# One adaLN block on one core: the distance bias of the maximum is made by GpSimd alone from the fourth head on

## The reference

```python
scores = jnp.einsum('bihd,bjhd->bhij', q, k)
pos = jnp.arange(t)
alibi = -jnp.abs(pos[None, :] - pos[:, None]).astype(scores.dtype)
scores = scores + slopes[:, None, None] * alibi
probs = jax.nn.softmax(scores.astype(jnp.float32), axis=-1).astype(scores.dtype)
out = jnp.einsum('bhij,bjhd->bihd', probs, v).reshape(b, t, e)
```

## Time and profile before

| | |
|---|---|
| timed executions | 583.66, 583.89, 580.77 us |
| median | 583.66 us |
| profiled execution | span 580.7 us; its own time is taken as the 580.77 us above |
| TensorE busy | 457.7 us, 79% of the span |
| VectorE, ScalarE, GpSimd busy | 325.7, 255.4, 247.4 us |
| granted TensorE clock, mean of the span | 0.901 of full speed |

### The profile page before, as it was taken

The page is one execution under the profiler, slowest core; times in us unless marked ns, Lnnn a source line. Parts: engine busy times, 40 slices in busy tenths (PEclk is TensorE's granted clock), DMA queues, the critical chain, the costliest instruction groups (busy, mean ns, idle before and its releaser), DMA issues.

```text
span 580.7 us, 9712 instructions
## 1 busy us (share of the span) xinstructions
PE 457.7 (79%) x2167; PEld 233.9 (40%) x2168; DVE 325.7 (56%) x1035; ACT 255.4 (44%) x407; POOL 247.4 (43%) x351
## 2 busy tenths in 40 slices
PE   4988689999999999999988637976787777677800
PEld 1673133333333333333436623644444444344400
DVE  3836988888888888888514592332232232322336
ACT  1365347677666666666774411322222222222211
POOL 4584954333333333332300004455555555555523
PEclk9798669999999999999998656999889899989965
DMA  8439274233322222233210201111111111122065
GB/s 227 186 82 316 73 266 142 84 95 94 91 91 91 89 94 93 95 96 88 72 34 2 73 1 41 51 57 58 54 61 47 55 55 52 57 63 46 19 197 165
DMA packets 29407, 53.02 MB, mean 91 GB/s; under 512 B 5144, under 2 KB 14030, under 8 KB 29383
## 3 DMA queue, kind: packets, MB, share of 16 engines
q1 hardware_dynamic: 20119, 30.35, 15.8%
q0 software_dynamic: 8720, 21.87, 13.0%
q10 hardware_dynamic: 544, 0.53, 0.3%
HBM read 38.47 MB, written 16.22 MB: 94 GB/s over the span
## 4 chain that ended last, share of the span: by engine, by line
PE 43%; issue 21%; DVE 12%; POOL 11%; DMA 7%; POOLq 2%; ACT 1%; SPq 1%; DVEq 0%; ACTq 0%
PE ps L1341 11%; PE ps L1377 10%; PE ps L1354 8%; POOL probs L883 7%; PE ps L1495 3%; PE ps L1400 3%; DVE junk L992 2%; PE ps L1236 2%; DMA probs<-xn_rows,probs 2%; DVE x_sb L1197 2%; DMA x_sb<-in_x 2%; POOL probs L880 1%; POOL z_rows L893 1%; DMA k_st<-z_rows 1%; POOL probs L890 1%
## 5 line engine op out<-in xcount | busy, mean ns | idle before, releaser
L992 DVE CUSTOM_DVE_ANT_0 junk<-ps,bias_t 128x512 bf16<-128x512 f32 x256 | 172.4, 687 | 49.2 <-PE ps L1341 47.4
L638 ACT ACTIVATE probs<-ps 128x1024 f32<-128x1024 f32 x128 | 130.4, 1025 | 80.5 <-DVE ps L1016 36.6
L1341 PE MATMUL ps<-k_st,q_st 96*128 96x512 bf16 x256 | 102.9, 405 | 19.0 <-DVE mx L992 12.3
L1495 PE MATMUL ps<-w_gu,probs 128*128 x188 | 86.8, 588 | 0.0
L1354 PE MATMUL ps<-q_st,k_st 123*128 123x512 bf16 x256 | 78.4, 388 | 1.6 <-DMA q_st<-m_rows 1.4
L1377 PE MATMUL ps<-probs,v_st 128*32 128x512 f32 x512 | 68.4, 607 | 0.6 <-ACT probs L638 0.6
L1182 DVE TENSOR_TENSOR probs<-probs,ps 128x224 f32<-128x224 f32 x47 | 18.2, 388 | 90.0 <-ACT probs L714 90.0
L1341 PEld LDWEIGHTS ps<-k_st,q_st 96*128 96x128 bf16 x256 | 26.1, 102 | 105.3 <-DVE mx L992 87.0
L883 POOL DMA_INDIRECT probs<-xn_rows,probs x47 | 48.7, 1035 | 41.8 <-POOL probs L880 31.0
L703 ACT ACTIVATE probs<-ps,modc 128x128 f32<-128x128 f32 x47 | 21.5, 457 | 102.0 <-PE ps L1479 102.0
L893 POOL DMA_INDIRECT z_rows<-probs x47 | 48.5, 1033 | 41.8 <-POOL probs L890 37.9
(11 more groups left out here) (195 smaller groups left out, 626.2 us busy)
## 6 DMA issues: line engine op xcount, KB each, us to landing
k_st<-k_rows SPq DMA_DIRECT2D x32, 192.0 KB
w_gu<-in_gate_proj POOLq DMA_DIRECT2D x16, 224.0 KB, 3.1
w_gu<-in_up_proj POOLq DMA_DIRECT2D x16, 224.0 KB, 3.5
w_dn<-in_down_proj POOLq DMA_DIRECT2D x16, 224.0 KB, 3.5
q_st<-q_rows SPq DMA_DIRECT2D x16, 192.0 KB
k_st<-z_rows SPq DMA_DIRECT2D x4, 512.0 KB, 5.8
al_rows<-w_gu SPq DMA_DIRECT2D x1, 1536.0 KB, 9.1
k_st<-al_rows SPq DMA_DIRECT2D x32, 48.0 KB
```

The source lines that it names most:

```text
L638: act.activation(probs[:, j % 4, :], ps_st[j % 2].rearrange("p b n -> p (b n)"), ACT.Exp).then_inc(exp_done, 1)
L992: dve.tensor_tensor_reduce(junk[:, half, :], ps_max[half], bias_t[:, g % 2, off:off + CH], 1.0, -3.0e38, ALU.add, ALU.max, mx[:, g % 2, q, ...
L1341: pe.matmul(ps_max[half], q_st[0:R_QK, s, q * P:q * P + P], k_st[0:R_QK, 0, s, CH * half:CH * half + CH], start=True, stop=True).then_inc( ...
L1495: last = pe.matmul(ps[:, 2 + c % 2, 0:2 * INTER], xT[:, c % 2, kk, :], w_gu[:, bass.ds(e, 1), kk, :].rearrange("p x n -> p (x n)"), start= ...
```

## The change

From the fourth head on, GpSimd makes all 1920 columns of the bias in one operation. ScalarE's two operations per step are gone, and VectorE waits only for GpSimd's semaphore before the first maximum of such a head. The first three heads stay as they were.

```diff
@@ ScalarE, step(i, c)
                     if output and j == 1:
                         evac_o(i, c - 1)
-                    if j in (3, 5) and (not isinstance(i, int) or 0 <= 4 * i + c and 4 * i + c + 3 < H):
-                        make_bias_t(i, c + 3, (j - 3) // 2)
                     if rows and j == 4:
                         evac_rows(i, c + 1)
@@ GpSimd, make_bias_p(i, c)
                 s = c % 2
-                w = 2 * W_DIST // 3
                 pool.wait_ge(max_used, at(i, c - 1, k=16))
                 settle(pool)
-                pool.tensor_scalar(bias_t[:, s, w:], dist[:, w:], slope_now[:, s, :], None, ALU.mult).then_inc(bias_p_done, 1)
+                pool.tensor_scalar(bias_t[:, s, :], dist[:], slope_now[:, s, :], None, ALU.mult).then_inc(bias_p_done, 1)
@@ VectorE, step(i, c)
                         if q == 0:
-                            dve.wait_ge(bias_t_done, at(i, g, k=2) + 2)
                             if is0(i):
+                                dve.wait_ge(bias_t_done, 2 * g + 2)
                                 dve.wait_ge(bias_a_done, g + 1)
                             else:
                                 dve.wait_ge(bias_p_done, at(i, g) - 2)
```

## The result

The changed kernel takes 641.32 us in the median of four runs (640.67 to 642.89); the kernel before took 583.77 us (580.77 to 584.64). The ratio is 1.1006, with a 95% interval from 1.0962 to 1.1051. The change makes the kernel 10% slower. Forecast were 597.6 us and a range up to 618 us.

What follows compares the result with a forecast made beforehand. Steps are bound by TensorE, which waits for VectorE's maximum behind line 1035. Longer holds of 12.8 us in steps 1 to 12 plus 1.1 us in step 0 raise the 583.66 us median to 597.6 us; range 583 to 618 us.

Steps and rivals of the forecast that it cites:

- The bound: Head steps: TensorE busy 14.18 of 14.7 us; its idle 0.5 us includes a 0.3 us wait for VectorE's maximum.
- ScalarE's 21.3 us: Two ScalarE operations of 0.82 us removed in 13 steps; covered by TensorE's work, so valued at nothing.
- GpSimd's operation: Bias operation grows from 640 to 1920 columns, to 5.11 us, 3.23 us more; by its length alone costs nothing.
- The hold: Line 1035, held by GpSimd's bias operation, ends 1.07 us later in steps 1 to 12: 12.8 us; chance 0.60.
- the line: VectorE's hold from GpSimd's start: 0.28 us plus 0.83 ns a column, so 1.88 us for 1920 columns.
- pieces: GpSimd works columns in pieces, first one 1024: line 1035's hold 0.32 us longer, 588 us in all; chance 0.11.
- the second rival: VectorE held for GpSimd's whole operation: line 1035 at 4.9 us, 4.3 us more a step, 640 us; chance 0.10.
- All of the 1.07 us reaches TensorE: VectorE runs without a gap from line 1035 to TensorE's awaited maximum, so the longer hold fully delays TensorE.
- TensorE's clock: Changed kernel's profile would show TensorE's clock granted in full, at 1.00, as in the step shown before.
- the wait of 1.4 us: TensorE's wait behind line 1035 in the changed kernel would be near 1.4 us, in a step of 15.8 us.
- Step 0: Line 1033 held 1.07 us longer, line 1034 perhaps to GpSimd's end: 1.1 us taken, bounds 0.7 and 3.0.
- The late row: Row of maxima returns late behind weight loads: TensorE waits 1.4 us more in 12 steps, 17 us, 614 us; chance 0.06.

Runs made afterwards that it cites:

- The two runs with the meeting avoided: GpSimd's bias waits until the fourth split operation ends: in the changed kernel (1920 columns) 575.89 us, 0.9885; in the kernel before (640) 575.84 us, 0.9897.
- the ratio of 0.9969: Kernel before, from the fourth head on without ScalarE's two bias parts, GpSimd still at 640 columns: 579.65 us.
- three operations in a row: Changed kernel with GpSimd's 1920 columns as three operations of 640, VectorE waiting for all three: 582.19 us, ratio 0.9978.
- The nine rows of holds: Table of VectorE's hold for GpSimd operations of 640 to 1920 columns, from the kernel before, the changed one and follow-up runs: 0.81 to 3.63 us.
- with the clock kept up: Changed kernel with 12 unused TensorE multiplications before the score matmul that waits for VectorE, in steps 1 to 12: 615.7 us, ratio 1.06.

## Why the prediction was wrong

**The bound, right.** A step is bound by TensorE, and the one place where TensorE waits is behind line 1035. The two runs with the meeting avoided show it: 0.5 and 0.4 us a step.

**ScalarE's 21.3 us, nearly right.** Valued at nothing, they are worth 1.8 us by the ratio of 0.9969, with an interval from 0.3 to 3.3 us. That the 1920 columns behind the split, without ScalarE's parts, and the 640, with them, have the same median says the same.

**GpSimd's operation, right.** 5.12 us for 5.11, and nobody waits for the bias, the diagonal bias or the weights: three operations in a row cost nothing.

**The hold, wrong in size.** The step that failed is "For 1920 columns the line gives 0.28 + 1.60 = 1.88 us, so line 1035 would end 1.88 - 0.81 = 1.07 us later". That VectorE is held at this meeting, and where, was right, but the line was drawn from lengths up to 1024 to almost the double, and it ends between 1088 and 1152 columns. Measured: 3.63 us, 2.82 us later than before, instead of 1.07. I had named pieces and put their bound at +0.32 us, because I took VectorE to be let in after the first piece. The nine rows of holds fit another reading: it is let in only after the last column is read, so that a second piece adds the whole working time of the first. That this is how GpSimd works is inferred; the holds themselves are measured. The case "a third of a long operation may need more room than the chip keeps" was in the text, under the second rival, but priced with the hold to the end.

**"All of the 1.07 us reaches TensorE", right.** 2.82 us of hold became 2.73 us of step, with the clock kept up.

**TensorE's clock, wrong.** The prediction says "TensorE's clock granted in full, at 1.00". No term of the sum stood for it, and it is 24 of the 57 us. No run has the wait of 1.4 us that was forecast. With waits of 0.6 to 0.7 us (1024 and 1088 columns) the clock was 1.00 in all twelve steps. With 2.5 to 2.6 us it was 1.00 in most (a step of 17.00 us with 1280 columns) and lower in three of twelve steps with 1152 columns and in two of twelve with 1216 and with 1280. With 2.9 us (1600 columns) it was lower in eleven, with 3.1 us in all twelve.

**Step 0.** The kernel after (1030 and 1031 are lines 1033 and 1034 of before), and the run with one operation of 1024 columns:

```profile
80.32 5.13 POOL L752 TENSOR_SCALAR bias_t<-dist,slope_now 128x1920 f32<-128x1920 f32 x1 [0.24 <-POOL slope_now L744]
...
80.70 3.25 DVE L1030 TENSOR_TENSOR m_rest<-negm,m_part 128x8 f32<-128x8 f32 x1
...
84.48 0.99 DVE L1031 CAST m_part<-m_rest 128x8 bf16<-128x8 f32 x1
```
```profile
81.41 2.85 POOL L757 TENSOR_SCALAR bias_t<-dist,slope_now 128x1024 f32<-128x1024 f32 x1 [0.24 <-POOL slope_now L749]
...
83.07 0.16 DVE L1037 CAST m_part<-m_rest 128x8 bf16<-128x8 f32 x1
```

Line 1033 was held as line 1035 is (80.70 + 3.25 - 80.32 = 3.63 us), and the cast behind it to the end of GpSimd's operation (84.48 + 0.99 = 85.47 us against 80.32 + 5.13 = 85.45). The 1.1 us I took were 3.6, beyond the upper bound of 3.0. The cast is not held to the end in every run, though: with 1024 columns it starts 1.66 us behind GpSimd's start and 1.19 us ahead of its end, and takes 0.16 us; with 1088 columns (1.72 us behind) it also takes 0.16 us. With 640 (before), 1600 and 1920 columns it ends with GpSimd's operation. Why stays open.

**The second rival** gave 640 us, and the time is 641, but not by its mechanism. It wanted line 1035 at 4.9 us, and it lasts 3.43; the clock, which it did not have, makes up the difference. That is luck. A time that fits does not confirm the mechanism. **The late row** did not come: between 94 and 340 us TensorE's twelve waits, 37.5 us together, are all for VectorE's maximum. (Its price was a little off: 6.5 - 5.18 is 1.3 us a step and 16 us in all, not 1.4 and 17.)

The Trainium skill's rule in "SBUF — State Buffer", section "Who interferes with whom", that the second instruction "fully blocks", is borne out for VectorE's two-input operation only in part: it is held for 3.63 of the 5.12 us. For the cast in step 0 the trace of the kernel after agrees with it to the end, and the runs with 1024 and 1088 columns do not: there the cast is let through. Behind a GpSimd operation with two inputs the trace of the kernel before agrees with it for two inputs as well: line 1033 ends at 62.14 + 0.58 = 62.72 us, and the first of two GpSimd operations, 2.27 us together from 61.55, ends near 62.69.

## What to carry to other kernels

Before an operation on GpSimd is made longer, look in the timeline for VectorE operations with two SBUF inputs, or casts within SBUF, that start inside it: the first were held here in every such meeting shortly behind GpSimd's start, the casts in some. What counts is the length of the one operation that they meet, not GpSimd's total work, and a hold of 0.4 us on a tiny operation is already worth removing. Cut the GpSimd operation, or start it behind the small ones with one more wait; both cost nothing here, and the second made the kernel 0.8 to 1.1% faster. Don't extend a line beyond the lengths that the trace shows, and when a wait of TensorE grows, price the clock behind it as well as the wait.

## What was not expected of the hardware

VectorE's hold by a GpSimd operation with a scalar from memory jumps from 1.18 to 2.99 us between 1088 and 1152 columns, while GpSimd's own time goes evenly from 3.04 to 3.20 us. And with 3.1 us of idleness in each step TensorE's clock falls to 0.50 in each, and the mean clock of a step to 0.83 or 0.91, so that a step loses 2.03 us beside the 2.73 us of the wait itself.
